# One core, a four-layer gated stack with a 16-head attention: VectorE normalises both token tiles, and P.V becomes two plain fp32 products

## The reference

```python
def rmsnorm(x, g):
    return x * rsqrt(mean(x * x, -1) + eps) * g
q = rmsnorm(h @ Wq, gq)          # h: layernorm of the tokens, 256 x 256; 16 heads of 128
k = rmsnorm(ctx @ Wk, gk)        # ctx: context, 256 x 128
v = ctx @ Wv
p = softmax(q @ k.T / sqrt(128)) # per head 256 x 256
out = (p @ v) @ Wo               # summed over the heads
```

## Time and profile before

| | |
|---|---|
| median of 3 runs | 1250.54 us (1250.01 to 1252.74) |
| profiled execution, its own time | 1251.78 us |
| span of the profile, first to last instruction | 1249.6 us |
| busy: PE, PEld, DVE, ACT, POOL | 840.5, 618.9, 831.5, 493.4, 371.2 us |
| mean granted clock of TensorE, of 2.4 GHz | 0.812 |

### The profile page before, as it was taken

The page is one execution under the profiler, slowest core; times in us unless marked ns, Lnnn a source line. Parts: engine busy times, 40 slices in busy tenths (PEclk is TensorE's granted clock), DMA queues, the critical chain, the costliest instruction groups (busy, mean ns, idle before and its releaser), DMA issues.

```text
span 1249.6 us, 15616 instructions
## 1 busy us (share of the span) xinstructions
PE 840.5 (67%) x4052; PEld 618.9 (50%) x4052; DVE 831.5 (67%) x1944; ACT 493.4 (39%) x1242; POOL 371.2 (30%) x412
## 2 busy tenths in 40 slices
PE   2114863587338853785469797879789697888756
PEld 1003641465126621673256585657567485667535
DVE  4896789569875889467630596439863596439763
ACT  2421422224212422243137554545365454555332
POOL 4744362317322553212020122131123212131123
PEclk9555985689558965798589898989999897999857
DMA  3150000010001000023210000010000100000000
GB/s 130 67 233 13 0 1 1 1 47 0 0 0 47 0 0 0 18 84 139 78 53 22 13 1 6 1 35 1 4 1 0 35 0 5 0 21 1 1 0 9
DMA packets 12185, 33.43 MB, mean 27 GB/s; under 512 B 2120, under 2 KB 5584, under 8 KB 10320
## 3 DMA queue, kind: packets, MB, share of 16 engines
q1 hardware_dynamic: 12112, 32.70, 7.5%
HBM read 30.59 MB, written 2.10 MB: 26 GB/s over the span
## 4 chain that ended last, share of the span: by engine, by line
issue 48%; DVE 21%; POOL 14%; PE 10%; ACT 3%; DMA 1%; POOLq 1%; DVEq 1%; SPq 0%; ACTq 0%
PE bk L955 9%; DVE pool L1508 2%; POOL acl L589 2%; DVE pool L1514 2%; POOL pool L557 2%; POOL th L632 2%; POOL ac L595 2%; DVE t L1534 1%; DVE pool L1500 1%; DMA pool<-in_wo 1%; DVE mx L1708 1%; POOL lnr L529 1%; POOL fside L617 1%; POOL first L632 1%; DVE th L1722 1%
## 5 line engine op out<-in xcount | busy, mean ns | idle before, releaser
L557 POOL TENSOR_TENSOR pool<-pool 128x512 f32<-128x512 f32 x64 | 94.0, 1468 | 124.5 <-DVE pool L1514 124.2
L1534 DVE SCALAR_TENSOR_TENSOR t<-th,bk 128x256 f32<-128x256 f32 (+1 forms) x120 | 50.1, 418 | 107.0 <-ACT th L771 105.9
L955 PE MATMUL bk<-hT,first 128*128 128x256 f32 (+1 forms) x448 | 112.8, 399 | 0.0
L762 ACT ACTIVATE ssm_da<-m,nega 128x255 f32<-128x255 f32 x128 | 57.7, 499 | 118.3 <-DVE pool L1508 104.7
L955 PEld LDWEIGHTS bk<-hT,first 128*128 128x128 f32 (+1 forms) x448 | 87.9, 200 | 15.7 <-issue 1.0
L955 PE MATMUL bk<-early,first 128*128 128x256 f32 x384 | 94.8, 384 | 0.0
L955 PE MATMUL bk<-bc,sel 96*128 96x512 bf16 (+1 forms) x128 | 52.7, 418 | 58.2 <-DVE pool L1514 45.4
L1508 DVE TENSOR_TENSOR_SCAN pool<-ssm_da,pool 128x512 f32<-128x512 f32 x64 | 90.3, 1410 | 0.4
L632 POOL TENSOR_TENSOR th<-th,rd 128x256 f32<-128x256 f32 x48 | 29.4, 612 | 189.6 <-DVE rd L1718 189.6
L955 PE MATMUL bk<-first,ac 128*128 128x256 f32 (+1 forms) x224 | 64.8, 414 | 29.7 <-POOL ac L570 29.7
L771 ACT ACTIVATE th<-bk 128x256 f32<-128x256 f32 x88 | 33.9, 385 | 125.6 <-PE bk L955 125.3
(11 more groups left out here) (353 smaller groups left out, 2356.6 us busy)
## 6 DMA issues: line engine op xcount, KB each, us to landing
out<-xo SPq DMA_DIRECT2D x8, 256.0 KB, 2.5
pool<-in_wo SPq DMA_DIRECT2D x4, 512.0 KB, 4.7
first<-in_wq SPq DMA_DIRECT2D x1, 2048.0 KB, 9.1
first<-in_wd SPq DMA_DIRECT2D x1, 1792.0 KB, 16.7
first<-in_wg SPq DMA_DIRECT2D x1, 1760.0 KB, 8.7
first<-in_wu SPq DMA_DIRECT2D x1, 1760.0 KB, 12.5
xin<-in_x SPq DMA_DIRECT2D x4, 256.0 KB, 3.2
pool<-in_q3u SPq DMA_DIRECT2D x1, 1024.0 KB, 5.2
```

What stands on the lines that cost most here:

```text
L557: g.tensor_tensor(sy, sy, ssm_u[:, n % 3, :].rearrange("p (e t) -> p e t", e=2), ALU.add).then_inc(*sig("s0.pool", "y", n))
L762: i = s.activation(ssm_da[:, n % 2, e, 1:], sdl[:, e, 1:], ACT.Exp, scale=nega[:, e, n:n + 1])
L955: return t_.matmul(dst, lhsT, rhs, start=start, stop=stop)
L1534: v.scalar_tensor_tensor(out=quarter(t1, c)[0:m, :], in0=quarter(th, c)[0:m, :], scalar=1.0, in1=bank[0:m, 0:S], op0=ALU.add, op1=ALU.mult ...
```

## The change

GpSimd's `normalise` is gone, in the attention and in s6. DVE normalises both tiles, one after the other, in `rden`, and the transposes wait for DVE alone, tile by tile. The splits are gone: ACT's copy and DVE's subtraction for the context, and DVE's two subtractions per head. ACT copies the transposed probabilities in one instruction of 512 columns, unrounded, to the two tiles `pT4` (memory of `t1`). P.V is two fp32 products of 256 columns, and it and the transposes two heads on wait for ACT's copy in place of DVE's subtractions. The whole diff:

```diff
@@ build
-        pTh4 = [[hTh[:, 0, :], hTh[:, 1, :]], [ach[0][:, :], ach[1][:, :]]]
-        pTl4 = [[hTl[:, 0, :], hTl[:, 1, :]], [acl[0][:, :], acl[1][:, :]]]
-        cxh4, cxl4 = [t[2][:, :].rearrange("p (k c) -> p k c", k=2) for t in (ach, acl)]
         oT4 = [t[:, 0:S] for t in t2]
@@ gpsimd
-            def normalise(b, k, j):
-
-                pool.wait_ge(*at(b, f"{k}.dve", "rd", j))
-                pm = pm4[j % 3][:, 1, :]
-                g.tensor_tensor(pm, pm, rd4[:, j, 1:2].broadcast_to([P, S]), ALU.mult).then_inc(*sig(f"{k}.pool", "pn", j))
-
-            def attention(b):
-                for j in range(NH):
-                    normalise(b, "sa", j)
-
             def s6(b):
                 yield AT6["ln"]
                 ln(b, "s6")
-                yield AT6["exp"]
-                normalise(b, "s6", 0)
@@ gpsimd, phase_b
-                attention(b)
-
                 interleave(rest(b), *([s4((b, 1))] if ahead else []))
@@ scalar, probsT
-                if k == "s6":
-                    s.activation(pT4[0], halves(bank), ACT.Copy).then_inc(*sig("s6.act", "pT", j))
-                else:
-                    for kc in range(2):
-                        s.activation(pTh4[j % 2][kc], bank[:, kc * S:kc * S + S], ACT.Copy).then_inc(*sig("sa.act", "pT", j, kc))
+                s.activation(pT4[j % 2], halves(bank), ACT.Copy).then_inc(*sig(f"{k}.act", "pT", j))
@@ scalar, attention
-                act.wait_ge(dma_sem("loadC"), b * 16 + 16)
-                s.activation(cxh4, cx[:, :, :], ACT.Copy).then_inc(*sig("sa.act", "cx"))
@@ tensor, probsT
-                    pe.wait_ge(*at(b, "sa.dve", "pl", j - 2, 1))
+                    pe.wait_ge(*at(b, "sa.act", "pT", j - 2))
                 bank = PTB[j % 2] if k == "sa" else MB
-                for t, half in enumerate(("dve", "pool")):
-                    pe.wait_ge(*at(b, f"{k}.{half}", "pn", j))
+                for t in range(2):
+                    pe.wait_ge(*at(b, f"{k}.dve", "pn", j, t))
@@ tensor, attention
-                        pe.wait_ge(*at(b, "sa.dve", "pl", h0, 1))
-                        parts = [(cxh4, pTh4), (cxl4, pTh4), (cxh4, pTl4)]
+                        pe.wait_ge(*at(b, "sa.act", "pT", h0))
                         for kc in range(2):
-                            for q, (c4, p4) in enumerate(parts):
-                                m = mm(OPB[i % 2][:, 0:S], c4[:, kc, :], p4[h0 % 2][kc],
-                                       start=kc == 0 and q == 0, stop=kc == 1 and q == 2)
+                            m = mm(OPB[i % 2][:, 0:S], cx[:, kc, :], pT4[h0 % 2][:, kc, :], start=kc == 0, stop=kc == 1)
@@ vector, rden
-                v.tensor_scalar(pm[:, 0, :], pm[:, 0, :], rd4[:, j, 0:1], None, ALU.mult).then_inc(*sig(f"{k}.dve", "pn", j))
+                for t in range(2):
+                    v.tensor_scalar(pm[:, t, :], pm[:, t, :], rd4[:, j, t:t + 1], None, ALU.mult).then_inc(*sig(f"{k}.dve", "pn", j, t))
@@ vector, attention
-                dve.wait_ge(*at(b, "sa.act", "cx"))
-                v.tensor_tensor(cxl4, cx[:, :, :], cxh4.bitcast(F32), ALU.subtract).then_inc(*sig(K, "cl"))
                 scale_k(0)
                 scale_k(1)
...
-                    if 0 <= i - 2 < NH:
-
-                        m = i - 2
-                        dve.wait_ge(*at(b, "sa.act", "pT", m, 1))
-                        for kc in range(2):
-                            v.tensor_tensor(pTl4[m % 2][kc], PTB[m % 2][:, kc * S:kc * S + S], pTh4[m % 2][kc].bitcast(F32),
-                                            ALU.subtract).then_inc(*sig(K, "pl", m, kc))
```

## The result

| | before | after |
|---|---|---|
| median | 1250.78 us (1249.63 to 1252.83, 20 runs) | 1244.95 us (1243.69 to 1250.3, 20 runs) |
| span of the profiled execution | 1249.6 us | 1242.8 us |

A forecast was written before the change was run, and what follows sets the result against it. DVE and ACT's loop of 3.08 us was taken to set the step, PE 0.08 behind. Attentions 4.1, context's split 0.7 and s6 0.7 sum to 5.5 us: 1250.5 to 1245.0 (given as 1245.1), range 1242.6 to 1249.6.

The forecast's parts named there:

- What bounds the kernel: Attention's steady step before the change: DVE and ACT's loop of 3.08 us sets it, PE has 2.99 work and 0.08 stall.
- The pair: DVE's two normalisations per head: 0.62 us together, 0.60 for the loop (0.54 to 0.74), making the loop 2.95.
- The rival of 0.81 for each: Each DVE normalisation stays at 0.81 us, the loop becomes 3.81, and the kernel slows to 1295 us; chance 0.05.
- TensorE's step: PE's steady attention step after the change: 3.13 us without stall, above DVE's 2.95, so PE becomes the bound.
- The rival with eight fp32r slots: Plain fp32 P.V takes 0.94 us, not 0.86; the gain falls to 0.7, time 1249.8 us; chance 0.10.
- VectorE's idle ahead of the maxima: Sign in the trace: DVE idles before the maxima, ended by PE, growing over the heads as PE falls behind.
- The attention: Each of four attentions saves 0.45 us at its start and 0.58 from step 4 on: 1.03, together 4.1.
- the last normalisation ends 0.81 - 0.62 = 0.19 sooner: Start of each attention: besides two loops saving 0.26 us, the last normalisation ends 0.19 sooner, together 0.45.
- The context's split: Without DVE's subtraction the scaling of k comes 0.34 us sooner in the second and third attention, 0.7 in all.
- s6: PE's transposes start 0.19 us sooner with both normalisations on DVE, limited by ACT: 0.17 x 4 = 0.7.
- The clock rival: PE's clock rises a step later in each attention, costing 5.2 us: 1250.3 us, no change; chance 0.07.
- The longer steady step does not make the attention longer: From step 4 on an attention takes 44.37 us against 44.95 before, since it starts earlier and ends densely.

The follow-up runs named there:

- the move alone: Kernel before, with only GpSimd's normalisation moved to DVE, which does both tiles; three-part fp32r P.V and its subtractions stay: 1236.47 us, ratio 0.9896.
- GpSimd's product beside the pair: Changed kernel, with GpSimd also multiplying 128 x 256 numbers nobody reads, at the moment of its former normalisation: 1259.27 us, ratio 1.0071.
- the later split: Normalisation moved to DVE, three-part P.V kept, context's split put behind the first two scalings of k, against the kernel before: 1236.26 us, again 1234.49 us.

## Why the prediction was right

*What bounds the kernel.* Right: VectorE and ScalarE set the step and TensorE's own work was 0.08 less; the broadcast takes 0.11 to 0.12 and the stall of 0.08 vanished in the move alone. Leaving out half of P.V gave the other side: with TensorE relieved, the loop of 2.88 sets the step.

*The pair.* Forecast 0.60 for the loop, measured 703.30 - 702.76 = 0.54 in the first attention, the lower end given, so the loop is 2.88 and not 2.95. The prediction itself noted that the next operation may start 0.08 before the end of a record, and should have taken that off in full: 0.62 - 0.08. The rival of 0.81 for each is excluded by the 0.62 itself, and GpSimd's product beside the pair shows where the 0.81 came from.

*TensorE's step.* Forecast 3.13, measured 3.14 to 3.15. The plain P.V takes 0.86; the rival with eight fp32r slots, 0.94, fell. One sign came otherwise: VectorE's idle ahead of the maxima was to grow from head to head. In the first attention the maxima of ten heads still follow the normalisation without idle, 2.88 apart at first (709.06, 711.94, 714.82), while VectorE uses up the time by which TensorE is ahead. Only from 732.54 on does it stand, 0.17 each time, and that does not grow.

*The attention.* Forecast 0.45 at the start and 0.58 behind it, measured 0.82 and 0.27; 1.03 against 1.1 in sum. That the sum fits is luck: two errors nearly cancel. The start was undersized because two terms were: the two loops gave 0.38 and not 0.26, and the transposes saved 0.45 and not 0.19. The step that failed there: "the last normalisation ends 0.81 - 0.62 = 0.19 sooner". It took the pair as one event, where the wait is tile by tile. With a wait for both it is 0.19 to the hundredth (0.87 from reciprocal to transposes, before 1.06). The gain behind was oversized: 44.37 us forecast, 44.68 measured. Most of it lies in the twelve steps up to the transposes of step 16, 37.32 forecast and 37.59 measured: the group of step 4 takes 0.10 more while it waits for the second tile, and the others are 0.01 to 0.02 longer each.

*The context's split.* Forecast 0.34 twice, measured 0.45 and 0.35 in one profile, 0.41 and 0.22 in the other.

*s6.* Forecast 0.17 each, measured 0.29 in three, by the same tile-by-tile wait; 0.19 without it. The last batch's 0.46 came at 1.2 GHz (1.11 for the group after, 1.12 before), where the first tile's transposes last until the second tile is there.

*The sum.* The three parts together were forecast at 5.5 and came to 6.5 in the profile. The median moved by 5.8 in the first comparison and by 6.5 in the second, so that it met the forecast within 0.3 the first time is partly luck too.

*The clock rival* came true in part, at no cost. In the first attention the transposes and scores of step 2 ran at 1.2 GHz after the change, at 2.4 before it:

```profile
703.17 1.11 PE L1154 MATMUL bk<-ident,th 128*128 128x128 f32 x4 [0.67 <-DVE th L1697]
...
704.08 1.91 PE L932 MATMUL bk<-pool 128*128 128x256 f32 x4
```

It cost nothing there, because VectorE's loop sets these steps: the attention gains 1.11 like the others. Outside the attentions it moved more, see below.

*What the prediction did not ask.* It added up one bundle and found 5.5. Cut in two, the move is worth 14.2 and the plain product, on top of it, costs 8.5. TensorE's step grows from 2.99 to 3.14: from step 4 on an attention takes 44.68 us instead of 43.00, which makes 6.7 in four. The last s6, where the move alone had the higher clock, makes 2.1 more in these two profiles, and other stretches give some of it back. The sentence "The longer steady step does not make the attention longer" holds against the kernel before, whose last step was held up, not against what the move alone makes possible. What the plain product takes away, the subtractions, was hidden in the loop, as the prediction itself said, and with the move they hold up the last step no longer. So every part of its price was in the working, and only the comparison was missing.

## What to carry to other kernels

Price a bundle's parts apart, each against the kernel that has the other part: a gain can hide that half of it costs more than it frees. Relief is worth something only on the engine that sets the step; here the six fp32r products on TensorE, the new bound, became two plain ones that take 0.15 us more a step, to spare VectorE, which had room. And an instruction whose twin runs on GpSimd may be slower for that company: two in a row on VectorE took less (0.62) than one beside GpSimd's (0.81). Last, a gain that sits in the clock of a stretch has to be seen in a second profile of the same kernel before it is booked.

## What the runs showed of the hardware that I had not expected

- The plain fp32 product of 256 columns takes 0.432 us, and three fp32r products 0.353. So a plain product costs 3.7 fp32r products. The Trainium skill's page "FP8 and Floating Point Precision", section "TensorE Precision Notes", gives true fp32 four passes; by it a pass would take 0.108 (an estimate), less than an fp32r product's 0.118. No row shows the passes themselves.
- Where TensorE's clock rises differs between executions, also of one kernel. In s5 of the second batch the middle 12 us were granted 0.94 of full speed before and 0.82 with the move alone, and the stretch took 1.46 us longer. It does not go with the kernel: with the later split it was 0.94 in the first profile, and the same time as before to 0.01, and 0.82 in the second, 1.47 longer. In the last batch's s6 the three profiles of the move with the whole three-part P.V gain 2.6, 1.8 and 2.7 us, the two of the change 0.5 each; there the size varies, and the order does not. The window before (PE busy comes first, the granted clock is the third number from the end):

```profile
909.00:921.00 12.00, 12.00 (x61) 8.36 (x59) 9.49 (x25) 10.12 (x32) 4.92 (x7) 0.94 0.00 1
```

And with the move alone:

```profile
902.40:914.40 12.00, 12.00 (x56) 8.50 (x54) 8.13 (x22) 8.66 (x29) 4.91 (x7) 0.82 0.00 1
```

And the second profile with the later split:

```profile
900.70:912.70 12.00, 12.00 (x56) 8.44 (x55) 8.04 (x22) 8.64 (x29) 4.91 (x7) 0.82 0.00 1
```

- VectorE's normalisation beside GpSimd's instruction ends 0.15 us behind it, in all 132 cases of the kernel before and of the run with the needless product.
- The last transfer lands 2.0 us behind its issue in eight profiles and 3.8 to 4.4 in the four that have a packet of the instruction queue beside it.
